# A clipped recurrence on VectorE, woven with its consumers in half steps, and 16-bit factors in a quantised SwiGLU

## The reference, cut to what matters

```
def step(carry, u):                       # L0_attn, 1024 steps in time
    sr, si = carry
    r, i = u
    sr = sr * decay + r * 0.1
    si = si * decay + i * 0.1
    nr = jnp.clip(sr * c - si * s, -10.0, 10.0)
    ni = jnp.clip(sr * s + si * c, -10.0, 10.0)
    return ((nr, ni), (nr, ni))

scores = einsum('bhqd,bhkd->bhqk', Q, K) / sqrt(dk)     # L0_xattn, 16 heads of 16
attn = softmax(scores, axis=-1)

# L1_ffn; act_qdq(x): scale = max(max|x| / 32767, 1e-12); clip(round(x / scale), -32768, 32767) * scale
x = act_qdq(x)
up = act_qdq(x @ lpbq_dequant(w_up).T)
gate = act_qdq(x @ lpbq_dequant(w_gate).T)
sig = fixed_qdq_u16(sigmoid(gate))        # clip(round(s * 65536), 0, 65535) / 65536
gate = act_qdq(gate * sig)
o = act_qdq(gate * up)
return o @ lpbq_dequant(w_down).T
```

## Time and profile before

| | |
|---|---|
| median of 3 runs | 2084.43 us |
| profiled execution | 2083.63 us |
| its span (first to last instruction) | 2081.8 us |
| mean granted TensorE clock | 0.92 |
| PE / DVE / ACT / POOL busy | 1778.3 / 1429.1 / 1046.0 / 451.8 us |
| scans and clips | 1024 each, 171 and 172 ns |
| first scan, last clip | 30.8 us, 522.5 us |
| first matmul of the ternary stage | 619.5 us |

### The profile page before, as it was taken

The page is one execution under the profiler, slowest core; times in us unless marked ns, Lnnn a source line. Parts: engine busy times, 40 slices in busy tenths (PEclk is TensorE's granted clock), DMA queues, the critical chain, the costliest instruction groups (busy, mean ns, idle before and its releaser), DMA issues.

```text
span 2081.8 us, 34894 instructions
## 1 busy us (share of the span) xinstructions
PE 1778.3 (85%) x12889; PEld 1267.9 (61%) x12889; DVE 1429.1 (69%) x4877; ACT 1046.0 (50%) x2606; POOL 451.8 (22%) x493
## 2 busy tenths in 40 slices
PE   3678888888879779999999999999879999989708
PEld 1356666666653455666667766666648989864307
DVE  6787888887235987767675676776536667653795
ACT  6544565454438535555553455555125545533852
POOL 4000000000000323333333333333212332320002
PEclk7768988898979979999999999999999999999859
DMA  5000000000000111000000000000413432400001
GB/s 155 1 1 1 2 1 1 1 1 1 1 1 15 26 22 66 1 2 1 1 1 1 1 1 1 2 1 1 134 42 81 93 90 65 92 1 0 0 0 41
DMA packets 86078, 49.56 MB, mean 24 GB/s; under 512 B 40223, under 2 KB 83669, under 8 KB 85717
## 3 DMA queue, kind: packets, MB, share of 16 engines
q1 hardware_dynamic: 80195, 47.18, 8.8%
q10 hardware_dynamic: 5714, 0.16, 0.2%
HBM read 45.24 MB, written 2.10 MB: 23 GB/s over the span
## 4 chain that ended last, share of the span: by engine, by line
PE 61%; DVE 24%; ACT 9%; issue 3%; POOL 2%; DMA 0%; ACTq 0%; POOLq 0%; DVEq 0%
PE PS L1661 7%; PE PS L1688 6%; DVE sq L742 6%; DVE nx L739 6%; PE PS L1962 6%; PE PS L1675 5%; PE PS L1646 3%; PE PS L1633 3%; PE PS L2375 3%; PE PS L2025 3%; PE PS L1703 2%; PE PS L1981 2%; PE PS L793 2%; PE PS L1990 2%; PE PS L1622 2%
## 5 line engine op out<-in xcount | busy, mean ns | idle before, releaser
L1727 ACT ACTIVATE px<-PS,cnm 128x128 f32<-128x128 f32 (+7 forms) x256 | 189.5, 741 | 261.7 <-DVE cnm L1775 254.7
L1818 POOL TENSOR_SCALAR px<-px,crl 128x128 f32<-128x128 f32 (+7 forms) x128 | 226.3, 1768 | 412.1 <-DVE crl L1790 412.1
L742 DVE TENSOR_SCALAR sq<-nx 128x4 f32<-128x4 f32 x1024 | 176.4, 172 | 35.2 <-DVE nx L739 0.2
L739 DVE TENSOR_TENSOR_SCAN nx<-sq 128x6 f32<-128x6 f32 x1024 | 174.6, 171 | 35.1 <-POOL sq L878 0.9
L1772 DVE TENSOR_REDUCE cm<-PS 128x1 f32<-128x128 f32 (+6 forms) x224 | 154.2, 688 | 55.0 <-PE PS L1661 54.5
L1675 PE MATMUL PS<-ident,px 128*128 128x128 f32 x1152 | 158.8, 278 | 14.3 <-ACT qT L1715 9.6
L1675 PEld LDWEIGHTS PS<-ident,px 128*128 128x128 f32 x1152 | 129.9, 141 | 61.5 <-issue 34.7
L1661 PE MATMUL PS<-kT,qT 64*128 64x512 f32 (+3 forms) x768 | 159.8, 521 | 5.0 <-ACT px L1727 2.6
L1688 PEld LDWEIGHTS PS<-pT,V 128*64 128x64 f32 x2304 | 124.9, 137 | 63.7 <-issue 34.6
L1688 PE MATMUL PS<-pT,V 128*64 128x128 f32 x2304 | 154.9, 279 | 5.9 <-DVE pT L1783 2.3
L2052 ACT ACTIVATE YT<-YT,xnm 128x154 f32<-128x154 f32 x256 | 104.8, 413 | 92.9 <-DVE xnm L2094 92.9
(11 more groups left out here) (340 smaller groups left out, 3910.3 us busy)
## 6 DMA issues: line engine op xcount, KB each, us to landing
xbs<-in_fside_Bx16xSxS SPq DMA_DIRECT2D x8, 1232.0 KB, 6.6
fsrc<-in_fside_Bx16xSxS SPq DMA_DIRECT2D x8, 1232.0 KB, 6.6
xmk<-in_mask_Bx16xSxS_bk SPq DMA_DIRECT2D x8, 308.0 KB, 8.3
fsrc<-in_mask_Bx16xSxS_bk SPq DMA_DIRECT2D x8, 308.0 KB, 8.3
X<-in_x SPq DMA_DIRECT2D x4, 512.0 KB, 6.8
w<-in_L_attn_W_ffn SPq DMA_DIRECT2D x2, 1024.0 KB, 12.8
t<-in_L_ffn_w SPq DMA_DIRECT2D x2, 1024.0 KB, 11.8
out<-xs SPq DMA_DIRECT2D x16, 128.0 KB, 1.7
```

The lines of the kernel that those rows point to most:

```text
L739: e.tensor_tensor_scan(k.nx[:, :], d0, d1, 0.0, ALU.mult, ALU.add).then_inc(sem("rec.scan"), 1)
L742: e.tensor_scalar(o, bass.AP(k.nx, 2, [[6, P], [0, 2], [3, 2]]), 10.0, -10.0, ALU.min, ALU.max).then_inc(sem("rec.clip"), 1)
L1727: e.activation(k.px[n % 2][:, h, 0:width], src, ACT.Exp, scale=-1.0, bias=k.cnm[:, n % 4, h:h + 1], accum_out=k.cl[:, n % 4, h:h + 1]).the ...
L1818: e.tensor_scalar(k.px[n % 2][:, 0, 0:width], k.px[n % 2][:, 0, 0:width], k.crl[:, n % 4, 0:1], None, ALU.mult).then_inc(sem("c.normal0"), 1)
```

## The change

1. A step of the recurrence is two entries of the order, `scan` and `clip`. After each of the two every chain is offered 0.5 steps, so that a step can be added between a scan and its clip. `k.nx` has two halves, used in turn.
2. `n.top` becomes 16 single steps per tile (12 of part 0, one group of heads each, and 4 of part 1), 0.5 apart; each reduces 154 scores. `n.normal` is split in `n.inverse` and `n.normal` (gap 0). The additions for the values are 10 steps and the ternary clips 2, at 0.5, in a chain of their own, the first 33.5 steps behind `n.value`.
3. `carry` goes: the last clip of a chunk is issued twice, first into the other half of `k.sq`, then into its own.
4. All gaps are new (table `GAPS`), and `LAST` is new: in it `t` stands once, as the last letter, and offers of the tail run steps with gaps up to 1 together.
5. SwiGLU: ScalarE writes the rounded `G` and `U` as int16 in one pass (no magic number), VectorE turns the sigmoid into uint16 and multiplies 16-bit operands into float32. `f.up` has no VectorE part any more.

```diff
-LAST = ("nusunuennsuesunsunusnuenuununnnuunsteststsutsutsuusueuuuuue")
+LAST = "ueueessnsunsnussnnnusuueununuennnnnssssssussusuueuuuut"
...
-        for n in range(C if c < BT else 0):
-            o.add(("rec", c * C + n))
...
-            net.offer(1)
-            scores.offer(1)
-            sums.offer(1)
-            ends.offer(1)
+        other = Chain(o, needs, first_chunk(third, x0) if c == 1 else ())
+        for n in range(2 * C if c < BT else 0):
+            o.add((("scan", "clip")[n % 2], c * C + n // 2))
+            for chain in (net, scores, sums, ends, other):
+                chain.offer(0.5)
...
+def first_chunk(third, x0):
+    yield 4, ("tern_int",)
+    yield GAPS["value"] - 4, ("n.value", 0)
+    yield 0, ("n.value", 1)
+    for b in range(B):
+        for i in range(5):
+            yield GAPS["piece"] if b + i == 0 else 0.5, ("n.piece", b, i)
+    for n in range(2):
+        yield 0.5, ("tern_clip", n)
+    for n in third:
+        if n not in x0:
+            yield 0, ("flip", n)
+
+GAPS = dict(value=26.5, piece=33.5, f0=3.5, f0l=8, sum1=14, shift1=6.5, turn1=4.5, up0=4.5, up=5.5, down0=6.5, down1=2, sum2=8.5, sum2l=17, shift2=6, turn2=16.5,
+            turn2l=5, score=11, score1=2, top=18, top3=0.5, peak=7, mix=23, spread=11.5, normal=16.5, inv=0, back=0, out=3, sum3=18, shift3=33, r3=4.5)
...
     def offer(self, passed):
+        close = 1 if passed >= 100 else 0
...
-            if self.left:
+            if self.left > close:
                 return
+            if close:
+                self.left = 0
...
-    yield 5, ("n.score", T, 0)
-    yield 23, ("n.top", T, 0)
-    yield 0, ("n.score", T, 1)
-    yield 6, ("n.top", T, 1)
-    yield 0, ("n.peak", T)
+    yield g["score"], ("n.score", T, 0)
+    for i in range(12):
+        yield 0.5 if i else g["top"], ("n.top", T, i)
+    yield g["score1"], ("n.score", T, 1)
+    for i in range(12, 16):
+        yield 0.5 if i > 12 else g["top3"], ("n.top", T, i)
+    yield g["peak"], ("n.peak", T)
...
-    yield 27, ("n.mix", T)
-    yield 8, ("n.spread", T)
-    yield 20, ("n.normal", T)
-    yield 4, ("n.back", T)
-    yield 4, ("n.out", T)
+    yield g["mix"], ("n.mix", T)
+    yield g["spread"], ("n.spread", T)
+    yield g["normal"], ("n.inverse", T)
+    yield g["inv"], ("n.normal", T)
+    yield g["back"], ("n.back", T)
+    yield g["out"], ("n.out", T)
...
-        e.tensor_tensor_scan(k.nx[:, :], d0, d1, 0.0, ALU.mult, ALU.add).then_inc(sem("rec.scan"), 1)
+        e.tensor_tensor_scan(k.nx[:, t % 2, :], d0, d1, 0.0, ALU.mult, ALU.add).then_inc(sem("rec.scan"), 1)
+
+    def clip(t):
...
         w.wait_ge("rec.scan", t + 1)
-        o = bass.AP(k.sq, base + 7, [[4 * W6, P], [W6, 2], [3, 2]])
-        e.tensor_scalar(o, bass.AP(k.nx, 2, [[6, P], [0, 2], [3, 2]]), 10.0, -10.0, ALU.min, ALU.max).then_inc(sem("rec.clip"), 1)
-
-    def carry(c):
-        w.wait_ge("rec.clip", c * C)
-        w.wait_ge("rec.out", c - 1)
-        if c < BT:
-            e.tensor_copy(k.sq[:, c % 2, :, 1:5:3], k.sq[:, (c - 1) % 2, :, 6 * C + 1:6 * C + 5:3]).then_inc(sem("rec.carry"), 1)
+        if n == C - 1 and c < BT - 1:
+            e.tensor_scalar(place((c + 1) % 2 * 2 * W6 + 1), state, 10.0, -10.0, ALU.min, ALU.max).then_inc(sem("rec.carry"), 1)
+        e.tensor_scalar(place(c % 2 * 2 * W6 + 6 * n + 7), state, 10.0, -10.0, ALU.min, ALU.max).then_inc(sem("rec.clip"), 1)
...
-            if part:
-                dst, src = k.nnm[:, 3, j, 0:1], PS[:, 4 + j, 0:S2]
-            else:
-                dst, src = k.nnm[:, 0:3, j, 0], PS[:, 4 + j, 0:3 * S2].rearrange("p (m s) -> p m s", m=3)
-            e.tensor_reduce(dst, src, AX.X, ALU.max, negate=True).then_inc(sem("n.max"), 1)
+        e.tensor_reduce(k.nnm[:, m, j, 0:1], PS[:, 4 + j, m % 3 * S2:(m % 3 + 1) * S2], AX.X, ALU.max, negate=True).then_inc(sem("n.max"), 1)
...
-    ahead = 3
+    ahead, second = LANES, 2
     o.add(("f.acc", 3), ("f.gm", 3), *[("f.up", v) for v in range(ahead)], ("f.step", 3))
+    o.add(*[("f.second", v) for v in range(second)])
     for v in range(PARTS):
+        if v + second < PARTS:
+            o.add(("f.second", v + second))
+        o.add(("f.times", v))
         if v + ahead < PARTS:
             o.add(("f.up", v + ahead))
-        o.add(("f.times", v))
...
+    def sixteen(v):
+        w.wait_ge("f.sigmoid", v + 1)
+        e.tensor_scalar(k.sq16[:, v % 3, :, :], k.sg[:, v % 3, :, :], 65536.0, 65535.0, ALU.mult, ALU.min).then_inc(sem("f.sixteen"), 1)
...
-        e.tensor_scalar(sg, sg, 65535.0 / 65536.0, 192.0, ALU.min, ALU.add).then_inc(sem("f.value"), 1)
-        w.wait_ge("f.value", 2 * v + 1)
-        e.scalar_tensor_tensor(g, sg, 192.0, g, ALU.subtract, ALU.mult).then_inc(sem("f.value"), 1)
+        e.scalar_tensor_tensor(g, k.sq16[:, v % 3, :, :], 1.0 / 65536.0, k.gq[:, v % 3, :, :], ALU.mult, ALU.mult).then_inc(sem("f.value"), 1)
...
-    def up_(v):
-        w.wait_ge("f.tu", v + 1)
-        e.tensor_scalar(part(k.U, v), part(k.U, v), MAGIC, None, ALU.subtract).then_inc(sem("f.uq"), 1)
...
-        e.scalar_tensor_tensor(g, g, MAGIC, part(k.U, v), ALU.subtract, ALU.mult).then_inc(sem("f.value"), 1)
+        e.tensor_tensor(g, k.gq[:, v % 3, :, :], k.uq(v), ALU.mult).then_inc(sem("f.value"), 1)
...
-        e.activation(g, g, ACT.Identity, scale=s(6), bias=up).then_inc(sem("f.gq"), 1)
-        w.wait_ge("f.gq", 2 * v + 1)
-        e.activation(g, g, ACT.Identity, bias=down).then_inc(sem("f.gq"), 1)
...
+        e.mul(q, part(k.G, v), s(6)).then_inc(sem("f.gq"), 1)
...
-        e.activation(u, u, ACT.Identity, scale=s(7), bias=up).then_inc(sem("f.tu"), 1)
...
+        e.mul(k.uq(v), part(k.U, v), s(7)).then_inc(sem("f.tu"), 1)
...
-        e.activation(g, g, ACT.Identity, scale=s(8), bias=up).then_inc(sem("f.t3"), 1)
+        e.mul(k.gq[:, v % 3, :, :], part(k.G, v), s(8)).then_inc(sem("f.t3"), 1)
```

More of the change, by code:

```diff
@@ L10 @@
 U8 = mybir.dt.uint8
+I16 = mybir.dt.int16
+U16 = mybir.dt.uint16
 ALU = mybir.AluOpType
@@ L577, in opening_tensor @@
     return {"spectrum": spectrum}
-LAST = ("nusunuennsuesunsunusnuenuununnnuunsteststsutsutsuusueuuuuue")
+LAST = "ueueessnsunsnussnnnusuueununuennnnnssssssussusuueuuuut"
 def recurrence_order(k):
     o = k.order
+    steps = lambda first, last: [(kind, j) for j in range(first, last) for kind in ("scan", "clip")]
     for d in range(DC):
@@ L620, in recurrence_order @@
         o.add(*together(*[[(kind, 0, T0 + lane) for kind in ("sum", "mean", "square", "root", "shift", "side", "turn", "put")] for lane in range(LANES)]))
-    o.add(*[("rec", j) for j in range(85)])
+    o.add(*steps(0, 85))
     o.add(("spectrum", 1))
@@ L626, in recurrence_order @@
     o.add(("tails",))
-    o.add(*[("rec", j) for j in range(85, 108)])
+    o.add(*steps(85, 108))
     o.add(("tern_scale",))
-    o.add(("rec", 108))
+    o.add(*steps(108, 109))
     o.add(("tern_inverse",))
@@ L634, in recurrence_order @@
     o.add(*[("n.key", m) for m in range(4)])
-    o.add(*[("rec", j) for j in range(109, C)])
-    o.add(("carry", 1), ("rec_out", 0), ("rec_in", 2))
+    o.add(*steps(109, C))
+    o.add(("rec_out", 0), ("rec_in", 2))
     k.near_tiles = [b * BT + t for t in range(BT) for b in range(B)]
@@ L648, in recurrence_order @@
         net = Chain(o, needs, network_chain(c - 1))
-        for n in range(C if c < BT else 0):
-            o.add(("rec", c * C + n))
[L651 to L654, removed]
-            net.offer(1)
-            scores.offer(1)
-            sums.offer(1)
-            ends.offer(1)
+        other = Chain(o, needs, first_chunk(third, x0) if c == 1 else ())
[3 more added lines that the diff above has]
+                chain.offer(0.5)
         if c < BT:
-            o.add(("carry", c + 1), ("rec_out", c))
+            o.add(("rec_out", c))
             if c + 2 < BT:
@@ L668, in recurrence_order @@
         chains[name].offer(100)
+    while any(chain.step for chain in chains.values()):
+        for chain in chains.values():
+            chain.offer(100)
+def first_chunk(third, x0):
[12 more added lines that the diff above has]
+            turn2l=5, score=11, score1=2, top=18, top3=0.5, peak=7, mix=23, spread=11.5, normal=16.5, inv=0, back=0, out=3, sum3=18, shift3=33, r3=4.5)
 class Chain:
@@ L704, in norm @@
                 yield 0 if i else wait, (kind, L, T)
-    yield 7 if late else 8, ("from", 0, t)
+    g = GAPS
+    yield g["f0l"] if late else g["f0"], ("from", 0, t)
     yield 0, ("from", 1, t)
-    yield from norm(1, 3, 11, 0 if late else 13)
+    yield from norm(1, g["sum1"], g["shift1"], 0 if late else g["turn1"])
     for j in range(8):
[L709 to L712, removed]
+        yield g["up"] if j else g["up0"], ("up", t, j)
+    yield g["down0"], ("down", 0, t)
+    yield g["down1"], ("down", 1, t)
+    yield from norm(2, g["sum2l"] if late else g["sum2"], g["shift2"], g["turn2l"] if late else g["turn2"])
 def recurrence_vector(e, w, k):
@@ L723, in tern_inverse, with tern_clip, scan @@
```

(13 more changed lines are left out.)

77 lines of the change are left out of this document (49 added, 28 removed).

## The result

The kernel after took 2050.48 us (median of four runs, 2048.83 to 2051.84), the kernel before 2084.41 beside it (2083.91 to 2084.84): ratio 0.9837, 95% interval 0.982 to 0.9854. Forecast were 2043 us and 2031 to 2060; the direction and the range hold, and 7.5 us of the expected 41 are missing.

The account below looks back on a forecast made before the run. The prediction took VectorE as the bound of the recurrence, with TensorE just under it and bounding the tail. Recurrence -36.4, tail +4 and SwiGLU -8.8 summed to -41 us: 2043 us for the median, range 2031 to 2060.

Parts of the forecast that it names:

- Maxima, boundary, values: Recurrence: single maxima save 14.5 us, the dropped state copy 1.9, values and ternary clips in separate places 1.0; 17.4 us.
- The overlap behind a scan: Recurrence, VectorE: a single maximum overlaps a scan as it does a clip; assumed, since no row of before showed it.
- its rival (12 us, no overlap): Recurrence: nothing overlaps a scan, so half of the single maxima save nothing; +12 us, 2055 us; chance 0.08.
- The copy of the state: Chunk boundary: the copy goes, 0.27 us 7 times, 1.9 us saved; the second clip lies in the gap behind the first.
- Waits: Recurrence: of VectorE's 23.2 us of waits for scores and values, 4.2 us stay, 0.7 per chunk; 19.0 us saved.
- The forecast of the last clip (486): End of the recurrence: the last clip comes near 486 us instead of 522.7, 36.4 us less.
- Tail: Behind the recurrence: single maxima cost 0.54 us for each of two tiles, the ternary start is about 3 us late; +4 us.
- SwiGLU: SwiGLU stage at the end: a ScalarE pass and VectorE's subtractions for `U` go; 8.8 us less.
- The product in 16 bits: SwiGLU, VectorE: keeps 1.75 us; at twice the rate the time would be up to 6 us lower.
- TensorE as the bound: Recurrence: TensorE sets the chunk, six chunks at 59.2 us instead of 57.7; +9 us, 2052 us; chance 0.17.
- Slower: Recurrence: TensorE's low clock spreads and chunks grow; at 67 us per chunk the kernel takes 2099 us; chance 0.04.

Follow-up runs that it names:

- e9_later_tail_kept: Kernel after, with the last four maxima of each chunk's second tile placed later, except in tiles 14 and 15: 2044.63 us, ratio 0.9801 to the kernel before.
- e10_later_and_ternary: e9_later_tail_kept with the start of the ternary stage also spread over the tail: 2036.86 us, ratio 0.9766 to the kernel before.
- e6_ternary_beside_tail: Kernel after, with the start of the ternary stage spread over the tail by new letters in `LAST`: 2039.61 us, ratio 0.978 to the kernel before.

## Why the prediction came out right, and where it was off

The direction and the parts are right, and the range of 29 us was wide enough for the rest. In the profiled executions 7.0 us are missing: 3.4 in the recurrence, 2.1 in the tail, 2.9 in the ternary stage, less 1.4 more gained at the end.

*Maxima, boundary, values: 17.4 us of work expected, about 18 measured* (33.0 in all, less 14.5 of waits and 0.5 by which the first scan came earlier). The overlap behind a scan was the open point; the rows at 263.58 and 263.66 settle it, and its rival (12 us, no overlap) falls. The Trainium skill (VectorE: DVE Perf Modes, "The DRAIN you can't avoid") has the next operation start only when the pipe is empty, and adds that one which is not held starts earlier. The forecast's rival went by the first half alone. The trace agrees with the second: an independent instruction starts 0.08 us behind the start of a scan of 0.16. Dependent ones stand 0.205 us apart in both kernels. The copy of the state was put at 1.9 us, 7 times its 0.27; with what the second clip costs (0.07 each) it was 1.4.

*Waits: 19.0 us expected, 14.5 measured. This is the term of the recurrence that was mis-sized.* 23.2 us stood before, and I left 4.2; the recurrence of after has 8.7. I took 0.7 us of waiting per chunk from a comparison of totals (TensorE and VectorE level near 57.2). The traces have a wait of 0.9 to 1.15 at one instruction in each ordinary chunk, the thirteenth maximum of the second tile, and 1.16 and 2.46 us in the chunk from 140 to 200 us. It is no balance of engines: the later maxima removed nearly all of it and took 1.0 us off a chunk. The forecast of the last clip (486) lies between after (489.5) and that kernel (483.4; 483.6 with the tail kept).

*Tail: +4 expected, +6.1 measured.* The first ternary matmul starts 4.95 us behind the last output's start, in before 1.14: 3.8 us late where I had 3, and three waits for VectorE and ScalarE make 2.05 of them. The single maxima cost 0.5 us a tile as reckoned, but for all four tiles of the tail, not for two: wide ones there took 2.3 us off it.

*Ternary stage: not in the sum, +2.9 measured.* Its steps are the same. In thirteen kernels with the same steps there it takes 162.9 to 168.8 us; the forecast put at nothing what can move by some 5 us, and why it moves is open.

*SwiGLU: 8.8 expected, 9.5 measured* (the last scale step was 24.3 us early on entering and 33.85 on leaving: 2029.04 to 1995.19). The product in 16 bits keeps 1.75 us. By the Trainium skill (same page, "What auto-detection actually checks") the doubled rate wants all tensors in 16 bits, and the result is float32. The 1.75 us agree with that; no run here has all three in 16 bits.

*TensorE as the bound* (0.17, 2052 us) comes nearest in time, by 1.5 us, but not in kind: chunks were 57.7 and 56.7 us, not 59.2. *Slower* was not seen in after, and yet was nearer than I had it, through the table of places. With the network's old places the same order is no faster than before, with all of them (and the new letters in the tail) 35 us slower, and there the low clock did spread: that tail was granted 0.73, the tail of after 0.85. The forecast leaned on positions that I had only laid out on paper, for the order as written, and never asked what they were worth.

## What to carry to other kernels

When two engines look level, don't split the difference of their totals: find which single instruction waits in each period and for what, and move it by that wait; here 1 us at one maximum was 6 us of the kernel. Filling the gap between two dependent instructions with short independent ones pays on both sides of the pair: the maxima apart instead of in a row were worth 12.6 us of the recurrence. But the same finer steps took 2050, 2085 and 2121 us with three tables of places. And where an order is written as a string that is played against the state of several lists, any change of a gap upstream rewrites everything behind it: print the resulting order before measuring, and compare the tail step by step. And before reading a difference of 2 us off two traces, subtract where the stage began in each.

## What the hardware showed that I had not expected

The same instructions with the same waits take different times, depending on where they fall. From the first px transpose to the end, the twelve kernels with the new SwiGLU stage have one program, and in one profiled execution of each it takes 1287.2, 1288.4 or 1288.5, and 1291.3 or 1291.4 us, nothing between. One place where it arises, behind the same waits of 1.67 and 0.46 us; first after, then e9_later_tail_kept:

```profile
1459.94 0.44 PE L227 MATMUL PS<-ident,X 128*128 128x128 f32 x2 [1.67 <-DVE X L186]
1460.84 3.72 PE L1736 MATMUL PS<-WzT,YT 128*128 128x256 f32 x16 [0.46 <-ACT XT L291]
```

```profile
1450.92 0.44 PE L227 MATMUL PS<-ident,X 128*128 128x128 f32 x2 [1.67 <-DVE X L186]
1451.82 5.41 PE L1737 MATMUL PS<-WzT,YT 128*128 128x256 f32 x16 [0.46 <-ACT XT L291]
```

Sixteen matmuls take 3.72 us in one and 5.41 in the other; TensorE's mean granted clock over them is 1.00 in the first and 0.67 in the second, so part of them ran at the lower of its two levels, behind the same idle time. With the ternary stage's 162.9 to 168.8 us this makes gains of a few us come out up to some 5 us larger or smaller than at the place where they are made: e10_later_and_ternary kept 2.8 of 6.1, and e6_ternary_beside_tail gave 10.9 for 4.3. What in the position decides was not tried, nor how much of it differs between executions of one kernel, of which the four of after lie between 2048.8 and 2051.8 us.
